# Recurrent step of a four-layer graph network: the tanh of the gates goes to the cell's PSUM bank, and h times c gets a semaphore per half

## The chip, the cores and the metric

The kernel runs on one core of a Trainium2 chip. The metric is the device time in microseconds of one execution, the median of the runs of a kernel. The engines are named as in the profile: PE is TensorE, DVE is VectorE, ACT is ScalarE, POOL is GpSimd, SP is SyncE.

## What is computed

Four layers run one after the other on 6250 rows of 256 features, each as `x = x + layer(layernorm(x))`: a graph attention layer, a mixture of experts, a three-hop graph convolution, and a recurrent layer. The change touches only the recurrent one. It walks over the 6250 rows in order, with a batch of one, a hidden state `h` and a cell `c` of 256 values each:

```python
def step(carry, xs):
    h, c = carry
    xi_t, xf_t, xg_t, xo_t = xs
    i_t = jax.nn.sigmoid(xi_t + h @ V_i)
    f_t = jax.nn.sigmoid(xf_t + h @ V_f)      # not used by c_new
    g_t = jnp.tanh(xg_t + h @ V_c)
    o_t = jax.nn.sigmoid(xo_t + h @ V_o)
    c_new = h * c + i_t * g_t
    h_new = o_t * jnp.tanh(c_new)
    return ((h_new, c_new), h_new)
```

The old cell is multiplied by the old `h`, not by a forget gate. A step needs the `h` of the step before, so nothing of one step's gates can start before the step before has ended.

## The kernel before

`lstm_layer` keeps the 256 hidden values as two halves (`KD` = 2, index `m` or `q`) of 128 partitions by one column. All weights are split into a high and a low fp16 part, and a product takes three terms (high by high, low by high, high by low), so a step has 36 matmuls of 128x128 by 128x1: 24 for the gates `i` and `g` (banks `ZI0`, `ZI1`), then 12 for `o` (banks `ZO..`). `ORDER` sets their order by hand: bank `ZI0` (gates of half 0) is complete after 17 of them, `ZI1` after 24, the two `o` banks after 30 and 36. The parts `x @ U + b` of the next 125 steps are added ahead, one wide matmul after each of the first 48 steps of a group of 125.

The work of a step, half by half, each handed over by a semaphore that counts steps (`t`):

- PE (line 2402) waits for `h1_made[q]` (the high part of half q of `h`) and later `h2_made[q]` (its low part), and raises `z[bank]` with the last matmul of a bank.
- ACT (line 2419) waits for `z[m]` and writes the tanh of both `i/2` and `g` (two columns) to the SBUF tile `tg`; it raises `gates[m]`. The sigmoid of `i` is had from the tanh of half its argument.
- DVE (line 2446) waits for `gates[m]`, in half 0 for `hc_made` too, and makes the new cell by a scan of two columns from `tg` and `one_hc` (the columns 1 and h*c) into columns 0 and 1 of the PSUM tile `c[m]`, a bank for each half; it raises `cell[m]`.
- ACT (lines 2422 and 2424) makes the sigmoid of `o` (waits for `z[2 + m]`), then the tanh of the cell (waits for `cell[m]`), and raises `tanh_made[m]`.
- DVE (line 2451) multiplies the two into `h1`, the fp16 value that PE waits for. Then follow the low part (line 2455), `h` in fp32 (line 2456), and for the next step h*c of half 0 and of half 1 (lines 2458 and 2459), of which the second raises `hc_made`.

Each engine runs its own instructions in the order in which the code is written; the body of the loop is written out for 1250 steps and run five times. POOL copies `h` of 125 steps at a time to a table (line 2358). On steps 0 and 1 of each group of 125, ACT clears half a bank (line 2427).

In the built program an instruction carries one wait. Where the code has two, the wait that is written last becomes an instruction of its own (a semaphore instruction on the same queue) ahead of the one that works, and the wait that is written first stays on the working instruction. Another place with two waits is the expert layer, where one transpose on PE (line 1718) raises `transh`, and both DVE and ACT wait for that same semaphore, DVE with one wait and ACT with two:

```python
                        dve.wait_ge(transh, 2 + 2 * t + n + 1)      # 1771
                        nc.vector.tensor_copy(HT[:, ...], psT[n][:]...)                  # 1772
...
                        act.wait_ge(hid, 2 * t + n + 1)             # 1646, done long before
                        act.wait_ge(transh, 2 * t + n + 1)          # 1647, stands ahead on its own
                        nc.scalar.activation(Hs[:, ...], psH[...][:], ACT.Gelu)          # 1648
```

Of the kernel before, what the change touches and what calls it, by code (L numbers as in the profile page):

```python
# [8 lines left out]
ACT = mybir.ActivationFunctionType  # L9
ALU = mybir.AluOpType  # L10
AXX = mybir.AxisListType.X

P = 128
# [4 lines left out]
KD = D // P  # L18
# [2172 lines left out]
def lstm_layer(nc, k, X, U, V, b, out):  # L2191
# [3 lines left out]
    with Phase(nc, "ls") as ph:  # L2195
# [8 lines left out]
        h = ph.sb("h", [P, RECENT, KD])  # L2204
        h1 = ph.sb("h1", [P, RECENT, KD, 2], F16)
        h2 = ph.sb("h2", [P, RECENT, KD, 2], F16)
        none = ph.sb("none", [P, KD * HALF])
        tg = ph.sb("tg", [P, 2, KD, 2])
        to = ph.sb("to", [P, 2, KD, 2])
        one_hc = ph.sb("one_hc", [P, KD, 2])  # L2210


        with Phase(nc, "lp") as pp:
# [12 lines left out]
            scale = sc[:, 0:1].bitcast(F32)  # L2226
            with pp.block() as block:
                @block.sync
                def _(sp):
                    sp.dma_start(Us[:], U.rearrange("(k p) (m c) -> p k m c", k=KD, c=P)).then_inc(loaded, 16)  # L2230
                    sp.dma_start(Vs[:], V.rearrange("(k p) (m c) -> p k m c", k=KD, c=P)).then_inc(loaded, 16)
                    sp.dma_start(brow[:], b.rearrange("(a m c) -> a m c", a=1, c=P)).then_inc(loaded, 16)
# [103 lines left out]
        with Phase(nc, "lr") as pr:  # L2336
            ZI = [pr.ps(f"ZI{m}") for m in range(KD)]
            ZO = [[pr.ps(f"ZO{i}{m}") for m in range(KD)] for i in range(2)]
            c = [pr.ps(f"c{m}") for m in range(KD)]
            cleared = [pr.sem(f"cleared{m}") for m in range(KD)]  # L2340
            z = [pr.sem(f"z{g}") for g in range(BANKS)]
            gates, cell, tanh_made, h1_made = ([pr.sem(f"{n}{j}") for j in range(KD)] for n in ("gates", "cell", "tanh", "h1_"))
            h2_made = [pr.sem(f"h2_{j}") for j in range(KD)]
            h_made, hc_made, kept = (pr.sem(n) for n in ("h", "hc", "kept"))

            def place(hf, bank, col, count):
                if bank < KD:
                    return ZI[bank][:, hf * KD * HALF + col:hf * KD * HALF + col + count]
                return ZO[hf][bank - KD][:, col:col + count]

            with pr.block() as block:
# [57 lines left out]
                @block.scalar  # L2409
                def _(act):  # L2410
                    back = act.alloc_register("unscale")
                    act.reg_load(back, sc[0:1, 1:2])
                    nc.scalar.preload_act_table(ACT.Sigmoid)
                    with act.Fori(0, N // BODY) as i:
                        for s in range(BODY):
                            hf, col, t = s // HALF % 2, s % HALF * KD, i * BODY + s
                            for m in range(KD):
                                act.wait_ge(z[m], t + 1)
                                nc.scalar.activation(tg[:, s % 2, m, :], place(hf, m, col, 2), ACT.Tanh, scale=back).then_inc(gates[m], 1)  # L2419
                            for m in range(KD):  # L2420
                                act.wait_ge(z[2 + m], t + 1)
                                nc.scalar.activation(to[:, s % 2, m, 1:2], place(hf, KD + m, col, 1), ACT.Sigmoid, scale=back)  # L2422
                                act.wait_ge(cell[m], t + 1)
                                nc.scalar.activation(to[:, s % 2, m, 0:1], c[m][:, 1:2], ACT.Tanh, scale=0.5).then_inc(tanh_made[m], 1)  # L2424
                            if s % HALF < KD:
                                m = s % HALF
                                nc.scalar.copy(place(1 - hf, m, 0, KD * HALF), none[:]).then_inc(cleared[m], 1)

                @block.vector
                def _(dve):  # L2430

                    nc.vector.memset(h1[:, 0:RECENT - 1], 0.0)
                    for m in range(KD):
                        nc.vector.memset(h1[:, RECENT - 1, m], 0.0).then_inc(h1_made[m], 1)
                        nc.vector.memset(h2[:, RECENT - 1, m], 0.0).then_inc(h2_made[m], 1)
                    nc.vector.memset(one_hc[:, :, 0], 1.0)
                    nc.vector.memset(one_hc[:, :, 1], 0.0).then_inc(hc_made, 1)
                    with dve.Fori(0, N // BODY) as i:
                        for s in range(BODY):
                            t, e, r = i * BODY + s, s % 2, s % RECENT  # L2440
                            for m in range(KD):
                                dve.wait_ge(gates[m], t + 1)
                                if m == 0:
                                    dve.wait_ge(hc_made, t + 1)

                                nc.vector.tensor_tensor_scan(c[m][:, 0:2], tg[:, e, m, :], one_hc[:, m, :], 1.0, ALU.mult, ALU.add).then_inc(cell[m], 1)  # L2446
                            if s % HALF == 0:
                                dve.wait_ge(kept, i * (BODY // HALF) + s // HALF + 1)
                            for m in range(KD):
                                dve.wait_ge(tanh_made[m], t + 1)  # L2450
                                nc.vector.tensor_tensor(h1[:, r, m, 1:2], to[:, e, m, 1:2], to[:, e, m, 0:1], ALU.mult).then_inc(h1_made[m], 1)  # L2451

                            for m in range(KD):
                                dve.wait_ge(h1_made[m], t + 2)
                                nc.vector.tensor_tensor_scan(h2[:, r, m, :], to[:, e, m, :], h1[:, r, m, :], 1.0, ALU.mult, ALU.subtract).then_inc(h2_made[m], 1)  # L2455
                            nc.vector.tensor_tensor(h[:, r, :], to[:, e, :, 1], to[:, e, :, 0], ALU.mult).then_inc(h_made, 1)  # L2456
                            dve.wait_ge(h_made, t + 1)
                            nc.vector.tensor_tensor(one_hc[:, 0, 1:2], h[:, r, 0:1], c[0][:, 1:2], ALU.mult)  # L2458
                            nc.vector.tensor_tensor(one_hc[:, 1, 1:2], h[:, r, 1:2], c[1][:, 1:2], ALU.mult).then_inc(hc_made, 1)  # L2459


        with Phase(nc, "lf") as pf:
# [71 lines left out]
def build(nc, x, src, dst, edge_weight, gat_W_src, gat_W_dst, gat_att_src, gat_att_dst, gat_bias, gat_gamma, gat_beta,  # L2534
          gat_prelu, moe_Wr, moe_br, moe_g, moe_b, moe_W1, moe_b1, moe_W2, moe_b2, gnn_WnT, gnn_bn, gnn_WsT, gnn_bs,
          lstm_U, lstm_V, lstm_b, out):
    with Phase(nc, "all") as ph:
        k = Constants(nc, ph)
        X = ph.sb("X", [P, NB, D])
        with ph.block() as block:  # L2540
            @block.vector
            def _(dve):
                nc.vector.memset(X[:, FULL:NB, :], 0.0)
        order = EdgeOrder(nc, "ss", src, dst, edge_weight)
        gat_layer(nc, k, x, X, src, dst, gat_W_src, gat_W_dst, gat_att_src, gat_att_dst, gat_bias, gat_gamma, gat_beta, gat_prelu, order)
        moe_layer(nc, k, X, moe_Wr, moe_br, moe_g, moe_b, moe_W1, moe_b1, moe_W2, moe_b2, order,
                  lambda Y, where, weight: gnn_layer(nc, k, X, order, gnn_WnT, gnn_bn, gnn_WsT, gnn_bs, Y, where, weight))
        lstm_layer(nc, k, X, lstm_U, lstm_V, lstm_b, out)
# [26 lines left out]
```

## Time and profile before

| | us |
|---|---|
| median of three runs | 19581.66 |
| lowest and highest run | 19550.09 and 19586.31 |
| span of the profiled execution, first to last instruction | 17545.4 |
| recurrent loop within that span | about 8147 to 17502 |
| one step of the loop, 6250 of them | 1.48 in most |

The profiled execution is one run; for its own time the profile gives the span alone, and the runs are about 2036 us longer than the span, which lies before the first and behind the last instruction that the profile counts. Engines are busy at the same time, so their shares do not add up. In the rows below, busy time is followed by the mean of one instruction; the last part of a row is how long its engine sat idle before it and what ended that.

### The profile page before, as it was taken

The page shows a single profiled execution, that of the slowest core. Times are in us where ns is not written, and L with a number is a line of the kernel's source. Part 1 is how long each engine was busy: PE and PEld are TensorE (multiplying, and loading weights), DVE is VectorE, ACT ScalarE, POOL GpSimd, SP SyncE. Part 2 cuts the span into 40 slices and gives each one's busy share as a digit, 9 for nine tenths or more (in the row PEclk, how much of TensorE's full clock was granted, in tenths as well). Part 3 has the DMA queues.
Part 4 walks back from the last instruction along what each step waited for, and adds up shares of the span by engine and source line. Part 5 has one row for each costly group of instructions (what it writes and reads, how often), then busy time and mean ns, then how long its engine had stood idle before and what let it go on. Part 6 is the DMA issues. An engine that isn't in the chain of part 4 may idle for free. (4 is left out here: it accounts for less than half of the span.)

```text
span 17545.4 us, 683245 instructions
## 1 busy us (share of the span) xinstructions
PE 12730.7 (73%) x250869; PEld 10213.3 (58%) x250870; DVE 11697.3 (67%) x68713; ACT 5986.8 (34%) x41949; POOL 5631.1 (32%) x6174
## 2 busy tenths in 40 slices
PE   5247773399655656556888888888888888888887
PEld 3135552266444544445777777777777777777776
DVE  7368887322555454556777777777777777777777
ACT  0004442011100101003555555554555555555555
POOL 4778887666576575772000000000000000000000
PEclk6558886599877777775555555555555555555555
DMA  0102222111333333331000000000000000000000
GB/s 22 25 21 73 74 72 43 56 34 33 101 105 98 96 105 87 105 105 37 4 4 4 4 4 4 4 4 4 4 4 4 4 4 4 4 4 4 4 4 18
DMA packets 352412, 609.44 MB, mean 35 GB/s; under 512 B 157501, under 2 KB 232222, under 8 KB 348988
## 3 DMA queue, kind: packets, MB, share of 16 engines
q0 software_dynamic: 223104, 471.33, 10.4%
q1 hardware_dynamic: 126524, 100.27, 1.9%
q8 instruction: 1835, 30.06, 0.7%
q14 instruction: 949, 7.77, 0.1%
HBM read 508.72 MB, written 62.45 MB: 33 GB/s over the span
## 5 line engine op out<-in xcount | busy, mean ns | idle before, releaser
L2402 PE MATMUL lr_ZI<-ls_h,ls_V 128*128 128x1 f16 x150000 | 5006.8, 166 | 1669.7 <-DVE ls_h L2451 1412.8
L2402 PEld LDWEIGHTS lr_ZI<-ls_h,ls_V 128*128 128x128 f16 x150000 | 4487.3, 104 | 2677.0 <-DVE ls_h L2451 2640.4
L2419 ACT ACTIVATE ls_tg<-lr_ZI 128x2 f32<-128x2 f32 x12500 | 2150.0, 172 | 4626.5 <-PE lr_ZI L2402 4534.6
L2446 DVE TENSOR_TENSOR_SCAN lr_c<-ls_tg,ls_one_hc 128x2 f32<-128x2 f32 x12500 | 2118.1, 170 | 1441.0 <-ACT ls_tg L2419 1317.8
L2358 POOL COPY ls_HT<-ls_h 128x250 f32 x50 | 19.8, 395 | 9358.3 <-DVE ls_h L2456 9358.3
L2402 PE MATMUL lr_ZO<-ls_h,ls_V 128*128 128x1 f16 x75000 | 2865.0, 165 | 0.0
L671 PE MATMUL prop_sum<-prop_G,prop_S 128*128 128x256 f32 x4992 | 1830.4, 546 | 1369.9 <-DMA prop_G<-hop_table,prop_idx 1369.9
L657 POOL DMA_INDIRECT prop_G<-hop_table,prop_idx x2496 | 2368.3, 949 | 1057.3 <-issue 708.8
L2402 PEld LDWEIGHTS lr_ZO<-ls_h,ls_V 128*128 128x128 f16 x75000 | 2483.2, 104 | 0.0
L671 PEld LDWEIGHTS prop_sum<-prop_G,prop_S 128*128 128x128 f32 x4992 | 1403.9, 288 | 1796.3 <-issue 1486.1
L2451 DVE TENSOR_TENSOR ls_h<-ls_to 128x1 f16<-128x1 f32 x12500 | 2023.4, 162 | 479.1 <-ACT ls_to L2424 16.0
L2424 ACT ACTIVATE ls_to<-lr_c 128x1 f32<-128x1 f32 x12500 | 2102.5, 169 | 9.9 <-DVE lr_c L2446 1.0
L2422 ACT ACTIVATE ls_to<-lr_ZO 128x1 f32<-128x1 f32 x12500 | 2069.3, 171 | 0.0
L2455 DVE TENSOR_TENSOR_SCAN ls_h<-ls_to,ls_h 128x2 f16<-128x2 f32 x12500 | 1633.5, 162 | 25.7 <-issue 25.7
L694 DVE TENSOR_TENSOR gnn_agg<-gnn_agg,prop_sum 128x256 f32 x1664 | 694.9, 418 | 908.7 <-PE prop_sum L671 884.9
L2458 DVE TENSOR_TENSOR ls_one_hc<-ls_h,lr_c 128x1 f32<-128x1 f32 x6250 | 969.0, 155 | 220.0
L633 ACT CAST prop_idx<-gnn_SRT 128x8 int32 (+1 forms) x312 | 63.3, 203 | 2915.2 <-DMA prop_G<-hop_table,prop_idx 2903.7
L680 DVE TENSOR_SCALAR prop_S<-all_cols,prop_lw 128x128 f32<-128x128 f32 x2520 | 900.5, 358 | 165.6 <-issue 153.3
L2456 DVE TENSOR_TENSOR ls_h<-ls_to 128x2 f32<-128x2 f32 x6250 | 952.9, 152 | 7.2 <-issue 7.2
L2459 DVE TENSOR_TENSOR ls_one_hc<-ls_h,lr_c 128x1 f32<-128x1 f32 x6250 | 930.2, 149 | 0.0
L522 POOL DMA_INDIRECT sd_records<-sc_rec,sc_place x784 | 772.5, 985 | 440.7 <-issue 408.0
L1007 POOL DMA_INDIRECT all_X<-gat_table,gs_idx x832 | 825.3, 992 | 239.1 <-issue 239.1
(455 smaller groups left out, 13965.7 us busy)
## 6 DMA issues: line engine op xcount, KB each, us to landing
prop_G<-hop_table,prop_idx POOLq DMA_INDIRECT x2496, 2.7
mow_W<-in_L_ffn_W SPq DMA_DIRECT2D x16, 1024.0 KB, 10.8
moe_out<-me_Ys SPq DMA_DIRECT2D x108, 128.0 KB, 1.7
all_X<-gat_table,gs_idx POOLq DMA_INDIRECT x832, 2.8
hop_table<-ht_T SPq DMA_DIRECT2D x50, 256.0 KB, 2.1
sd_records<-sc_rec,sc_place POOLq DMA_INDIRECT x784
ss_records<-me_recs,me_places POOLq DMA_INDIRECT x540
gat_table<-gt_hs SPq DMA_DIRECT2D x50, 128.0 KB, 1.8
```

The lines of the kernel that those rows point to most:

```text
L657: nc.gpsimd.indirect_dma_start(out=G[:, r, u, :], out_offset=None, in_=table[:, :], in_offset=bass.IndirectOffsetOnAxis(ap=idx[:, r, u:u + ...
L671: nc.tensor.matmul(ps[u][:, 0:D], S[:, r % 2, u, :], G[:, r, u, :], start=True, stop=True).then_inc(mm, 1)
L2402: mm = nc.tensor.matmul(place(hf, bank, col, 1), (V2 if part == "21" else V1)[:, q, ROWS.index(row), :], hx[:, prev, q, 1:2], start=False, ...
L2419: nc.scalar.activation(tg[:, s % 2, m, :], place(hf, m, col, 2), ACT.Tanh, scale=back).then_inc(gates[m], 1)
L2422: nc.scalar.activation(to[:, s % 2, m, 1:2], place(hf, KD + m, col, 1), ACT.Sigmoid, scale=back)
L2424: nc.scalar.activation(to[:, s % 2, m, 0:1], c[m][:, 1:2], ACT.Tanh, scale=0.5).then_inc(tanh_made[m], 1)
L2446: nc.vector.tensor_tensor_scan(c[m][:, 0:2], tg[:, e, m, :], one_hc[:, m, :], 1.0, ALU.mult, ALU.add).then_inc(cell[m], 1)
L2451: nc.vector.tensor_tensor(h1[:, r, m, 1:2], to[:, e, m, 1:2], to[:, e, m, 0:1], ALU.mult).then_inc(h1_made[m], 1)
L2455: nc.vector.tensor_tensor_scan(h2[:, r, m, :], to[:, e, m, :], h1[:, r, m, :], 1.0, ALU.mult, ALU.subtract).then_inc(h2_made[m], 1)
L2456: nc.vector.tensor_tensor(h[:, r, :], to[:, e, :, 1], to[:, e, :, 0], ALU.mult).then_inc(h_made, 1)
L2458: nc.vector.tensor_tensor(one_hc[:, 0, 1:2], h[:, r, 0:1], c[0][:, 1:2], ALU.mult)
L2459: nc.vector.tensor_tensor(one_hc[:, 1, 1:2], h[:, r, 1:2], c[1][:, 1:2], ALU.mult).then_inc(hc_made, 1)
```

## The change

`tg` goes away. The tanh of the gates is written to columns 2 and 3 (`GATED`) of the same PSUM tile `c[m]` whose columns 0 and 1 (`CELL`) hold the cell, and the scan reads it there. Since ACT now writes a bank that DVE reads in lines 2458 and 2459 (h*c), ACT waits for that h*c before it writes; for this `hc_made` becomes a list of two semaphores, one for each half.

```diff
-        tg = ph.sb("tg", [P, 2, KD, 2])
...
-            h_made, hc_made, kept = (pr.sem(n) for n in ("h", "hc", "kept"))
+            hc_made = [pr.sem(f"hc{j}") for j in range(KD)]
+            h_made, kept = pr.sem("h"), pr.sem("kept")
+            CELL, GATED = slice(0, 2), slice(2, 4)
...
                             for m in range(KD):
+                                act.wait_ge(hc_made[m], t + 1)
                                 act.wait_ge(z[m], t + 1)
-                                nc.scalar.activation(tg[:, s % 2, m, :], place(hf, m, col, 2), ACT.Tanh, scale=back).then_inc(gates[m], 1)
+                                nc.scalar.activation(c[m][:, GATED], place(hf, m, col, 2), ACT.Tanh, scale=back).then_inc(gates[m], 1)
...
                                 dve.wait_ge(gates[m], t + 1)
                                 if m == 0:
-                                    dve.wait_ge(hc_made, t + 1)
-
-                                nc.vector.tensor_tensor_scan(c[m][:, 0:2], tg[:, e, m, :], one_hc[:, m, :], 1.0, ALU.mult, ALU.add).then_inc(cell[m], 1)
+                                    dve.wait_ge(hc_made[KD - 1], t + 1)
+                                nc.vector.tensor_tensor_scan(c[m][:, CELL], c[m][:, GATED], one_hc[:, m, :], 1.0, ALU.mult, ALU.add).then_inc(cell[m], 1)
...
-                            nc.vector.tensor_tensor(one_hc[:, 0, 1:2], h[:, r, 0:1], c[0][:, 1:2], ALU.mult)
-                            nc.vector.tensor_tensor(one_hc[:, 1, 1:2], h[:, r, 1:2], c[1][:, 1:2], ALU.mult).then_inc(hc_made, 1)
+                            for m in range(KD):
+                                nc.vector.tensor_tensor(one_hc[:, m, 1:2], h[:, r, m:m + 1], c[m][:, 1:2], ALU.mult).then_inc(hc_made[m], 1)
```

No working instruction is added, dropped or moved on any engine; what changes is where two of them read and write, and the waits of one. The instructions of ACT for one step stand in the program before like this. A wait is shown under a name that its semaphore's number had in an earlier phase of the program: `gs_primed` is `z[0]`, `gs_ready` is `z[1]`, the others are `z[2]`, `cell[0]`, `z[3]`, `cell[1]`, in that order.

```order
L2418 REGISTER_ALU
L2419 ACTIVATE ls_tg<-lr_ZI0 128x2 [waits gs_primed]
L2419 ACTIVATE ls_tg<-lr_ZI1 128x2 [waits gs_ready]
L2422 ACTIVATE ls_to<-lr_ZO00 128x1 [waits gf_std_made]
L2424 ACTIVATE ls_to<-lr_c0 128x1 [waits gf_step]
L2422 ACTIVATE ls_to<-lr_ZO01 128x1 [waits gf_var_made]
L2424 ACTIVATE ls_to<-lr_c1 128x1 [waits gf_loaded]
```

The same step on ACT in the changed program; `mr_centred` is `hc_made[0]` and `mr_taken` is `hc_made[1]`. Of two names the first is the wait that stands as an instruction of its own ahead, the second is carried by the instruction shown.

```order
L2419 REGISTER_ALU
L2421 ACTIVATE lr_c0<-lr_ZI0 128x2 [waits gs_primed,mr_centred]
L2421 ACTIVATE lr_c1<-lr_ZI1 128x2 [waits gs_ready,mr_taken]
L2424 ACTIVATE ls_to<-lr_ZO00 128x1 [waits gf_std_made]
L2426 ACTIVATE ls_to<-lr_c0 128x1 [waits gf_step]
L2424 ACTIVATE ls_to<-lr_ZO01 128x1 [waits gf_var_made]
L2426 ACTIVATE ls_to<-lr_c1 128x1 [waits gf_loaded]
```

What moved is the wait for `z[m]`: from the tanh itself to a semaphore instruction ahead of it, while the new wait for h*c sits on the tanh. On DVE the new cell had two waits before and has them still, in the same places; `mr_taken` is `hc_made` of the kernel before, `gf_returned` and `gf_made` are `gates[0]` and `gates[1]`. Five instructions of DVE around it in the program before:

```order
L2456 TENSOR_TENSOR ls_h<-ls_to 128x2
L2458 TENSOR_TENSOR ls_one_hc<-ls_h,lr_c0 128x1 [waits mr_centred]
L2459 TENSOR_TENSOR ls_one_hc<-ls_h,lr_c1 128x1
L2446 SCALAR_TENSOR_TENSOR lr_c0<-ls_tg,ls_one_hc 128x2 [waits mr_taken,gf_returned]
L2446 SCALAR_TENSOR_TENSOR lr_c1<-ls_tg,ls_one_hc 128x2 [waits gf_made]
```

And in the changed program, where the same number on the first h*c has another old name (`h_made` in both):

```order
L2458 TENSOR_TENSOR ls_h<-ls_to 128x2
L2461 TENSOR_TENSOR ls_one_hc<-ls_h,lr_c0 128x1 [waits mr_prods]
L2461 TENSOR_TENSOR ls_one_hc<-ls_h,lr_c1 128x1
L2448 SCALAR_TENSOR_TENSOR lr_c0<-lr_c0,ls_one_hc 128x2 [waits mr_taken,gf_returned]
L2448 SCALAR_TENSOR_TENSOR lr_c1<-lr_c1,ls_one_hc 128x2 [waits gf_made]
```

Here nothing moved: the wait for h*c of half 1 stands alone ahead, and the wait for the gates is on the scan. (The scan is called SCALAR_TENSOR_TENSOR in this list and TENSOR_TENSOR_SCAN in the profile.)

## Rows read from the trace of the kernel before

**Rows 1.** The page: span, and granted TensorE clock in tenths, 40 slices
```profile
span 17545.4 us, 683245 instructions
...
PEclk6558886599877777775555555555555555555555
```

**Rows 2.** Waits in the loop, 8147.3 to 17502: total us, times, longest
```profile
ACT ls_tg L2419 <- PE lr_ZI L2402: 4534.6, 6250, 10.1
...
DVE lr_c L2446 <- ACT ls_tg L2419: 1317.8, 6105, 11.4
...
DVE ls_h L2455 <- issue: 25.7, 100, 0.3
```

**Rows 3.** Timeline of one step, all engines: start us, us, engine, line, what
```profile
12001.15 0.35 DVE L2451 TENSOR_TENSOR ls_h<-ls_to 128x1 f16<-128x1 f32 x2
...
12001.37 0.80 PE L2402 MATMUL lr_ZI<-ls_h,ls_V 128*128 128x1 f16 x24 [0.36 <-DVE ls_h L2451]
...
12001.80 0.16 DVE L2458 TENSOR_TENSOR ls_one_hc<-ls_h,lr_c 128x1 f32<-128x1 f32 x1
12001.87 0.15 DVE L2459 TENSOR_TENSOR ls_one_hc<-ls_h,lr_c 128x1 f32<-128x1 f32 x1
...
12002.02 0.36 ACT L2419 ACTIVATE ls_tg<-lr_ZI 128x2 f32<-128x2 f32 x2 [0.71 <-PE lr_ZI L2402]
...
12002.22 0.36 DVE L2446 TENSOR_TENSOR_SCAN lr_c<-ls_tg,ls_one_hc 128x2 f32<-128x2 f32 x2 [0.20 <-ACT ls_tg L2419]
12002.36 0.17 ACT L2422 ACTIVATE ls_to<-lr_ZO 128x1 f32<-128x1 f32 x1
12002.43 0.17 ACT L2424 ACTIVATE ls_to<-lr_c 128x1 f32<-128x1 f32 x1
...
12002.61 0.17 ACT L2424 ACTIVATE ls_to<-lr_c 128x1 f32<-128x1 f32 x1
12002.63 0.35 DVE L2451 TENSOR_TENSOR ls_h<-ls_to 128x1 f16<-128x1 f32 x2
...
12002.85 0.48 PE L2402 MATMUL lr_ZI<-ls_h,ls_V 128*128 128x1 f16 x12 [0.36 <-DVE ls_h L2451]
```

**Rows 4.** Line 2419: count, ns min/median/max, first and last start
```profile
L2419 ACT ACTIVATE ls_tg<-lr_ZI x12500: 172/172/173, 8147.3 to 17500.3; 128x2 f32<-128x2 f32 x199
```

**Rows 5.** Timeline of the expert layer, two places
```profile
3962.35 0.69 DVE L1772 COPY me_HT<-me_T 128x512 f32<-128x512 f32 x1 [1.75 <-PE me_T L1718]
3962.41 0.60 ACT L1648 ACTIVATE me_H<-me_H 128x512 f32<-128x512 f32 x1 [2.16 <-PE me_T L1718]
...
4397.55 0.69 DVE L1772 COPY me_HT<-me_T 128x512 f32<-128x512 f32 x1 [1.67 <-PE me_T L1718]
4397.61 0.60 ACT L1648 ACTIVATE me_H<-me_H 128x512 f32<-128x512 f32 x1 [2.27 <-PE me_T L1718]
```

**Rows 6.** Groups of ACT by line and shape: busy us, mean ns
```profile
L954 ACT CAST gs_ST<-gs_T 128x512 bf16<-128x512 f32 x208 | 110.8, 583 | 4.8 <-PE gs_T L1047 4.8
...
L2324 ACT COPY lp_xT<-lp_T 128x256 f32<-128x256 f32 x49 | 18.3, 373 | 12.5 <-PE lp_T L2307 11.6
L2087 ACT COPY co_idx<-moe_where 128x2 int32<-128x2 int32 x50 | 6.7, 183 | 12.3 <-PEq L72 12.3
...
L2427 ACT COPY lr_ZI<-ls_none 128x250 f32<-128x250 f32 x100 | 37.5, 375 | 0.0
```

**Rows 7.** Groups of DVE by line and shape: busy us, mean ns
```profile
L2446 DVE TENSOR_TENSOR_SCAN lr_c<-ls_tg,ls_one_hc 128x2 f32<-128x2 f32 x12500 | 2118.1, 170 | 1441.0 <-ACT ls_tg L2419 1317.8
...
L2455 DVE TENSOR_TENSOR_SCAN ls_h<-ls_to,ls_h 128x2 f16<-128x2 f32 x12500 | 1633.5, 162 | 25.7 <-issue 25.7
...
L1901 DVE TENSOR_TENSOR all_X<-all_X,ht_S 128x256 f32<-128x256 f32 x50 | 20.9, 420 | 54.9 <-PE ht_S L1975 54.9
...
L1147 DVE COPY gs_top<-gs_fin 128x4 f32<-128x4 f32 x104 | 19.0, 183 | 3.6
...
L772 DVE COPY gt_A<-gt_H 128x8 f32 x46 | 7.1, 154 | 0.0
...
L1906 DVE TENSOR_TENSOR ht_b<-ht_b 128x256 f32<-128x256 f32 x2 | 0.9, 426 | 12.3 <-DMA ht_b<-in_gnn_bs 12.3
```

More of the change, by code:

```diff
@@ L2436, in _ @@
                     nc.vector.memset(one_hc[:, :, 0], 1.0)
-                    nc.vector.memset(one_hc[:, :, 1], 0.0).then_inc(hc_made, 1)
+                    for m in range(KD):
+                        nc.vector.memset(one_hc[:, m, 1:2], 0.0).then_inc(hc_made[m], 1)
                     with dve.Fori(0, N // BODY) as i:
@@ L2457, in _ @@
                             dve.wait_ge(h_made, t + 1)
-                            nc.vector.tensor_tensor(one_hc[:, 0, 1:2], h[:, r, 0:1], c[0][:, 1:2], ALU.mult)
-                            nc.vector.tensor_tensor(one_hc[:, 1, 1:2], h[:, r, 1:2], c[1][:, 1:2], ALU.mult).then_inc(hc_made, 1)
+                            for m in range(KD):
+                                nc.vector.tensor_tensor(one_hc[:, m, 1:2], h[:, r, m:m + 1], c[m][:, 1:2], ALU.mult).then_inc(hc_made[m], 1)
         with Phase(nc, "lf") as pf:
```

## The prediction

> **What bounds the kernel now.** I read the page first: the span is 17545 us, and in its last 22 of 40 slices nothing of the granted clock changes; TensorE is granted 0.5 there, its lower level of 1.2 GHz [rows 1]. That stretch is the recurrent loop: its first and last tanh of the gates start at 8147.3 and 17500.3 us [rows 4], so 9353 us for 6250 steps, 1.497 us each, more than half of the span. The page's chain that ended last covers only the final addition and says nothing of the loop, so the waits come next: before every one of the 6250 steps ACT sits idle for PE (4534.6 us in total, 0.73 each), and DVE sits idle for ACT's tanh (1317.8 us) [rows 2]. No engine is full; a step is a chain of hand-overs. The timeline of one step shows it [rows 3]: DVE makes the two halves of the fp16 `h` from 12001.15 on; PE starts at 12001.37 with 24 matmuls, which run in 0.80 us; ACT starts the two tanhs at 12002.02 while the second bank is still being summed; DVE makes the cell from 12002.22 on; ACT does the sigmoids of `o` and the tanhs of the cell from 12002.36 on; DVE makes `h` again at 12002.63. From 12001.15 to 12002.63 is 1.48 us. PE takes 0.65 of it (12001.37 to 12002.02) and the four hand-overs ACT, DVE, ACT, DVE the rest. Every nanosecond added to the tanh of half 0 or to the scan behind it is therefore added to each step; the same holds for half 1, which runs 0.18 us behind in the same pattern, since PE needs it for its ninth matmul. The rest of 1.497 over 1.48 are longer steps, a few of them with DVE idle on issue (100 times, 25.7 us in total) [rows 2].
>
> One number decides whether the new wait can matter by itself. The h*c of half 0 starts at 12001.80 and lasts 0.16, so it is there at 12001.96, that of half 1 at 12001.87 + 0.15 = 12002.02, and the tanhs of the two halves start at 12002.02 and, 0.36 for two of 0.172 apart, at 12002.20 [rows 3, 4]. The h*c of each half is early by 0.06 and 0.18 us. So nothing has to wait for it for long; what it costs is the form in which the wait is built.
>
> **The change part by part.**
>
> *The wait of ACT.* In the changed program the tanh carries the wait for h*c, and the wait for `z[m]`, the one that comes last, stands ahead as an instruction of its own. Then ACT must first retire the semaphore instruction when `z[m]` rises and only then can bring up the tanh. The trace has that situation in the expert layer: DVE's copy and ACT's gelu wait for the same semaphore of the same transpose, DVE on the instruction and ACT on an instruction ahead of it. DVE starts at 3962.35 and 4397.55, ACT at 3962.41 and 4397.61 [rows 5], 0.06 us later in both; at a resolution of 0.01 I take 0.057. The opposite case is in the loop: the scan of half 0 has two waits as well, but there the one that stands ahead (h*c) has come long before. It starts at 12002.22, 0.03 behind the end of the tanh of half 0 (12002.02 + 0.172 = 12002.19), and the second scan, which has one wait, ends the pair at 12002.58 after a start at 12002.41, 0.03 behind the end of its tanh at 12002.38 [rows 3, 4, 7]. So a wait ahead is free when it is already met and costs 0.057 when it is the last. Bounds: 0 (as on that scan) and twice 0.057 (if the halves queued up behind each other). I take 0.057 once: the semaphore instruction of half 1 stands behind the tanh of half 0, which starts some 0.1 us before `z[1]` comes, so each half pays it, but side by side. Behind ACT's wait stand the sigmoid of `o` and the tanh of the cell; the sigmoid waits for PE, starts at 12002.36 now and has 0.16 us from the second tanh, so 0.04 more on that does not move it [rows 3]. On the wide matmuls that wait for `gates[m]` the delay falls into PE's idle time of 0.36 [rows 3].
>
> The Trainium skill ("Perfetto Trace Analysis", Identifying Dependency Chains) says that instructions which wait for several engines may have semaphore instructions put ahead of them. It gives no price; the trace agrees that the second wait is a thing of its own, by the 0.06 of [rows 5].
>
> *The tanh writes to PSUM.* No small instruction of ACT in the trace writes PSUM. The nearest is the clearing copy, SBUF to PSUM, 250 columns, 375 ns; PSUM to SBUF of 256 columns takes 373, of 512 columns 583, which makes 0.82 ns a column; SBUF to SBUF of 2 columns takes 183 [rows 6]. Without their columns: 375 - 205 = 170 to PSUM, 373 - 210 = 163 from PSUM, 183 - 2 = 181 for SBUF on both sides. So a PSUM destination in place of SBUF is worth 11 ns. Bounds: 0 (the wide copies differ by 2 ns only) and 18, the worth of a PSUM source. I take 11.
>
> The Trainium skill ("ScalarE: Activation LUTs", Step-by-step: what each stage is for) calls PSUM the destination of lower latency for ScalarE. It has no figure for it; the rows agree in sign, with the 11 ns above.
>
> *The scan reads PSUM.* An addition of 256 columns with one operand in PSUM takes 420 ns, one with both in SBUF 426; small copies take 154 from PSUM (8 columns) and 183 in SBUF (4 columns); against it, the scan that writes PSUM takes 170 where the one that writes SBUF takes 162, so PSUM is not the near side of DVE in every case [rows 7]. Bounds: 29 ns less and 8 more. I take 6 less, by the additions, which like the scan have two operands.
>
> *The semaphores of h*c.* DVE's first h*c now raises one itself. It is one increment by an instruction that is there already, and it lies in DVE's pause before the scan (0.20 idle) [rows 3]: nothing. That `tg` loses its two alternating buffers costs nothing either, since ACT reaches the next tanh only after it has waited for `cell[m]`, thus for the scan that read them. ACT has two more instructions to fetch per step, seven becoming nine; it sits idle 0.71 in each step, so a fetch is hidden. DVE has as many as before, PE too.
>
> *Sum.* 57 - 11 - 6 = 40 ns a step; times 6250 steps is 250 us. The profiled span would go from 17545 to 17795. The 2036 us that lie between the span and the median of the runs, 19581.66, are not touched, so the forecast is 19581.66 + 250 = 19832 us, 1.3% slower. Its own range: with no help from PSUM and 8 ns against, 65 ns, 406 us, 19988; with half of the price paid back (57 - 18 - 6 = 33 ns, 206 us) 19788; with all the help of the rows, 57 - 18 - 29 = 10 ns, 63 us, 19644.
>
> **The rivals.** From the measurement, about 0.2% (39 us, 6 ns a step) can be told from no change.
>
> *Faster: the wait ahead is hidden, PSUM pays.* If ACT brought the tanh up while the wait for `z[m]` is still open, as it seems on the first scan, the hop would be 0 and only the PSUM terms would be left: -17 ns, -106 us, 19476. It decides from the point where the hop costs less than the PSUM terms (17 to 47 ns). For it: the first scan's 0.03. Against it: that scan's leading wait was met long before, and where it is the last one, both places of [rows 5] show 0.06. 12 in 100.
>
> *No change: PSUM pays for the hop.* If both PSUM terms are at or near their far bounds, 47 ns, what is left is 10 ns or less; a scan that gains some more from reading and writing one bank would bring it to within 6 ns. The time would be 19582 to 19621. For it: the small copies differ by 29. Against it: the additions differ by 6. 9 in 100.
>
> *Slower still: both hops in a row.* If the semaphore instruction of half 1 could start only after the tanh of half 0 has been finished and not merely begun, half 1 would fall behind by a second 57 ns, and PE's ninth matmul and all behind would wait for it: 114 - 17 = 97 ns, 606 us, 20188. Against it: tanhs already start 0.18 apart with a length of 0.17, and half 1 of the chain has no need to be brought up earlier than 0.18 behind [rows 3, 4]. 4 in 100.
>
> **How the numbers follow.** Forecast with its own range (19644 to 19988) 75, faster 12, no change 9, slower still 4. The likeliest gives 19832. For 8 times in 10 the range goes from 19630, a little beyond the far bound of the PSUM terms, to 19990. Faster by over 0.2%: 12; within: 9; slower: 79.
>
> **What would show it.** In the changed profile the tanh of the gates should start about 0.057 later after PE's 24 matmuls began (now 0.65, then 0.71), the mean length of a tanh should fall from 172 to about 161, the scan from 170 to about 164, and a step should take 1.52 where it takes 1.48. The idle time of ACT for PE should rise by the hop, 0.057 a step, from 4534.6 to about 4890 us. PE's and DVE's parts should be the same. A step shorter than 1.48 would make the first term wrong, one over 1.57 the claim that the halves pay side by side. If the tanh's start has moved by 0.06 and the step has not grown, the two PSUM terms are mis-sized.

## The result

The changed kernel takes 19937.82 us in the median of four runs (19932.72 to 19945.11), the kernel before 19576.99 (19550.09 to 19586.31): a ratio of 1.0188, 95% interval 1.0174 to 1.0201. That is 361 us slower, 58 ns for each of the 6250 steps. The forecast was 19832, its range 19630 to 19990. Two of the eleven executions of experiment e1 below, at 19197 and 27441 us, were slow ones; every comparison here is of fast runs alone.

The page of the changed kernel, its span and the granted clock. Here the span is the time of the run but for 2 us, and in the loop, the last half of the slices, the clock is 0.5 as before:

```profile
span 19931.0 us, 695616 instructions
...
PEclk6555777657997676676655555555555555555555
```

The waits of the changed kernel in its loop (total us, times, longest), which answer to [rows 2]:

```profile
ACT lr_c L2421 <- PE lr_ZI L2403: 4925.4, 6254, 10.2
...
DVE lr_c L2448 <- ACT lr_c L2421: 1703.3, 6350, 11.5
ACT lr_c L2421 <- DVE ls_one_hc L2461: 82.8, 96, 0.9
```

ACT's idle time for PE has grown by 390.8 us and DVE's for ACT by 385.5 us; it is one loss, seen from two engines, and about what the kernel lost. The wait for h*c is the last one 96 times only. The tanh, the semaphore instruction ahead of it and the scan of the changed kernel (ns min/median/max, first and last start), which answer to [rows 4, 7]:

```profile
L2421 ACT ACTIVATE lr_c<-lr_ZI x12500: 157/157/157, 10159.4 to 19885.8; 128x2 f32<-128x2 f32 x199
...
L2420 ACTq EVENT_SEMAPHORE  x12500: 17/17/17, 10159.3 to 19885.7; - x199
...
L2448 DVE TENSOR_TENSOR_SCAN lr_c<-lr_c,ls_one_hc x12500: 157/170/170, 10159.6 to 19886.0; 128x2 f32<-128x2 f32 x199
```

The tanh takes 157 ns where it took 172; the scan takes 170 as before. From the first tanh to the last are 9726.4 us, against 9353.0 in [rows 4]: the loop lost 373 us. It starts at 10159 instead of 8147, though nothing ahead of it was changed; the section on the prediction comes back to that. One step of the changed kernel, which answers to [rows 3]:

```profile
14009.88 0.35 DVE L2453 TENSOR_TENSOR ls_h<-ls_to 128x1 f16<-128x1 f32 x2
14010.10 0.80 PE L2403 MATMUL lr_ZI<-ls_h,ls_V 128*128 128x1 f16 x24 [0.41 <-DVE ls_h L2453]
...
14010.53 0.22 DVE L2461 TENSOR_TENSOR ls_one_hc<-ls_h,lr_c 128x1 f32<-128x1 f32 x2
...
14010.82 0.34 ACT L2421 ACTIVATE lr_c<-lr_ZI 128x2 f32<-128x2 f32 x2 [0.78 <-PE lr_ZI L2403]
14011.01 0.36 DVE L2448 TENSOR_TENSOR_SCAN lr_c<-lr_c,ls_one_hc 128x2 f32<-128x2 f32 x2 [0.26 <-ACT lr_c L2421]
14011.10 0.17 ACT L2424 ACTIVATE ls_to<-lr_ZO 128x1 f32<-128x1 f32 x1
14011.21 0.17 ACT L2426 ACTIVATE ls_to<-lr_c 128x1 f32<-128x1 f32 x1
...
14011.41 0.35 DVE L2453 TENSOR_TENSOR ls_h<-ls_to 128x1 f16<-128x1 f32 x2
```

PE's first matmul to ACT's tanh is now 0.72 us, it was 0.65; a step (14009.88 to 14011.41, from DVE's product for `h1` to the next one) is 1.53, it was 1.48. The h*c of both halves is done at 14010.75, before the tanh starts. One more thing is to be read here: before, the tanh of the cell followed 0.07 behind the sigmoid of `o`; now it follows 0.11 behind it (14011.10 to 14011.21).

The trace also records when each semaphore rises. Times between such a record and the start of an instruction are given in ns below, as the median over the steps unless said otherwise. The tanh of half 0 starts 22 ns after `z[0]` rises in the kernel before and 88 ns after it in the changed one. That difference of some 65 ns is called the hop.

### The profile page after: what moved, and what is told of

Its sections match the earlier page's. It is cut to its first block and busy times, and to the rows that moved or that the text cites. A ratio compares the mean times of both kernels' runs of the same rounds, so it can differ in the third digit from the quotient of the medians.

```text
span 19931.0 us, 695616 instructions
## 1 busy us (share of the span) xinstructions
PE 13009.4 (65%) x250738; PEld 10113.7 (51%) x250870; DVE 11651.9 (58%) x68714; ACT 5778.6 (29%) x41949; POOL 5613.9 (28%) x6174
## 5 line engine op out<-in xcount | busy, mean ns | idle before, releaser
L2421 ACT ACTIVATE lr_c<-lr_ZI 128x2 f32<-128x2 f32 x12500 | 1955.4, 157 | 5187.8 <-PE lr_ZI L2403 4925.4
L2448 DVE TENSOR_TENSOR_SCAN lr_c<-lr_c,ls_one_hc 128x2 f32<-128x2 f32 x12500 | 2106.5, 170 | 1808.2 <-ACT lr_c L2421 1703.3
L671 PEld LDWEIGHTS prop_sum<-prop_G,prop_S 128*128 128x128 f32 x4992 | 1184.3, 259 | 2569.0 <-issue 2210.8
L2461 DVE TENSOR_TENSOR ls_one_hc<-ls_h,lr_c 128x1 f32<-128x1 f32 x12500 | 1385.6, 152 | 220.1
L638 ACT COPY prop_lw<-gnn_SRT 128x16 f32 (+1 forms) x315 | 64.4, 205 | 3472.5 <-DVE prop_S L680 2800.8
L1068 PE MATMUL gs_O<-gs_M,gs_S 128*128 128x260 f32 x1664 | 686.8, 503 | 138.9 <-issue 64.6
```

The lines of the kernel that those rows point to most:

```text
L671: nc.tensor.matmul(ps[u][:, 0:D], S[:, r % 2, u, :], G[:, r, u, :], start=True, stop=True).then_inc(mm, 1)
L2421: nc.scalar.activation(c[m][:, GATED], place(hf, m, col, 2), ACT.Tanh, scale=back).then_inc(gates[m], 1)
L2448: nc.vector.tensor_tensor_scan(c[m][:, CELL], c[m][:, GATED], one_hc[:, m, :], 1.0, ALU.mult, ALU.add).then_inc(cell[m], 1)
L2461: nc.vector.tensor_tensor(one_hc[:, m, 1:2], h[:, r, m:m + 1], c[m][:, 1:2], ALU.mult).then_inc(hc_made[m], 1)
```

## The experiments

All eight ran against the kernel before, which took 17554 us beside the first four (e1 to e4) and 17551 beside the last four, not 19577. The step of 1.48 us is read from the profiled run of the kernel before, whose span of 17545 us belongs to these times. The last column is of one profiled run each; single runs of the kernel before lie between 17544 and 17561 us, so differences of some 15 us in it mean nothing.

| run | what | ratio (95%) | us against before | loop, first to last tanh |
|---|---|---|---|---|
| kernel before, profile of before | | | | 9353.0 |
| e1 | one more wait, always met early | 1.0010 (1.0000 to 1.0019) | +13 | 9364.9 |
| e2 | the same, `z[m]` ahead | 1.0257 (1.0243 to 1.0271) | +454 | 9807.9 |
| e3 | changed kernel, waits swapped | 1.0034 (1.0021 to 1.0048) | +62 | 9422.0 |
| e4 | tanh in PSUM, in `ZI[m]` | 1.0005 (0.9996 to 1.0014) | +9 | 9365.0 |
| e5 | before, one `o` matmul less | 0.9996 (0.9987 to 1.0005) | -7 | 9368.0 |
| e6 | e4, one `o` matmul less | 0.9959 (0.9946 to 0.9973) | -70 | 9288.2 |
| e7 | changed kernel again | 1.0208 (1.0194 to 1.0222) | +369 | 9729.9 |
| e8 | e3 with an early h*c | 1.0002 (0.9993 to 1.0011) | +3 | 9366.2 |

### e1 and e2: the same two waits in both orders

The edit of e1 to the kernel before; e2 has the added line above the other one:

```diff
                                 act.wait_ge(z[m], t + 1)
+                                act.wait_ge(h2_made[m], t + 1)
```

> The kernel before, with one more wait on each tanh of the gates, on h2_made[m], written behind the wait for z[m], so that it stands ahead as an instruction of its own. h2_made of both halves comes some 0.29 us before z[0], so this wait is always met early. Theory (only a wait that comes last is dear when it stands ahead): the step stays at 1.48 us; two more instructions of ACT per step cost at most the 6 ns a step by which the changed kernel's mean outgrew its median, so 19577 to 19617. Rival (a second wait costs its 60 ns wherever it stands): 19577 + 6250 x 0.060 = about 19950.

> The same kernel as the one with the met wait, instruction for instruction, but with the wait for h2_made[m] written first, so that the wait for z[m], which comes last, stands ahead. The tanh still goes to SBUF. Theory: the whole loss of the changed kernel is this position, and its PSUM tile gives 15 ns a step back (tanh 172 to 157 ns): so this one is slower than the changed kernel, by 0.065 x 6250 = 406 us for the hop and up to 40 us for the two more instructions: 19980 to 20025. Rival (the loss comes from the PSUM bank or from waiting for h*c): near 19577.

Measured: e1 +13 us, e2 +454. The two kernels have the same instructions on every engine and differ in which of two waits stands ahead. Their tanhs and what follows, e1 first, both from the timeline:

```profile
12001.76 0.80 PE L2402 MATMUL lr_ZI<-ls_h,ls_V 128*128 128x1 f16 x24 [0.36 <-DVE ls_h L2452]
...
12002.41 0.36 ACT L2420 ACTIVATE ls_tg<-lr_ZI 128x2 f32<-128x2 f32 x2 [0.71 <-PE lr_ZI L2402]
```

```profile
12001.39 0.36 ACT L2420 ACTIVATE ls_tg<-lr_ZI 128x2 f32<-128x2 f32 x2 [0.78 <-PE lr_ZI L2402]
...
12001.67 0.17 ACT L2423 ACTIVATE ls_to<-lr_ZO 128x1 f32<-128x1 f32 x1
12001.80 0.17 ACT L2425 ACTIVATE ls_to<-lr_c 128x1 f32<-128x1 f32 x1
```

In e1 ACT's idle time before the tanh is 0.71 us, as without the extra wait [rows 3]; in e2 it is 0.78. By the semaphore records the tanh starts 23 ns after `z[0]` in e1 and 89 in e2, in the changed kernel 88. So the extra wait costs at most a few ns a step where the one ahead is met early (33 us at the end of the interval are 5 ns), and about 65 ns where the one ahead is the last to come: shown. It costs that once, not once a half: twice would have been over 800 us. And e2, with the hop and without the PSUM tile, is slower than the changed kernel in e7 by 454 - 369 = 85 us, 14 ns a step; that is close to the 15 ns by which the tanh is shorter when it writes PSUM.

### e3 and e8: the changed kernel with its waits in the other order

```diff
-                                act.wait_ge(hc_made[m], t + 1)
                                 act.wait_ge(z[m], t + 1)
+                                act.wait_ge(hc_made[m], t + 1)
```

> The changed kernel with the two waits of the tanh in the other order: z[m] first, then hc_made[m], so that the wait for h*c stands ahead. In the changed trace the semaphore of half 0's h*c comes only about 32 ns before z[0]; the semaphore instruction needs 21 ns to start and the tanh follows 67 ns behind it, so the tanh of half 0 can start 56 ns after z[0], where it is 88 in the changed kernel and 23 in the one before. Theory (position of the wait that comes last, and this latency): +33 for the rest of the hop, -15 for the tanh, -3 in the tanh of the cell, +6 for the longer queue = +21 ns a step, 130 us, about 19705. Rival A (a wait written last is free if it is met at all by z[m]): -12 ns a step, about 19500. Rival B (the order is not what costs): about 19940.

Measured: +62 us, half of the theory's 130 and far from both rivals. The swap alone takes back 307 of the 369 us. The tanh of e3:

```profile
12001.22 0.80 PE L2403 MATMUL lr_ZI<-ls_h,ls_V 128*128 128x1 f16 x24 [0.36 <-DVE ls_h L2453]
...
12001.63 0.22 DVE L2461 TENSOR_TENSOR ls_one_hc<-ls_h,lr_c 128x1 f32<-128x1 f32 x2
...
12001.89 0.32 ACT L2421 ACTIVATE lr_c<-lr_ZI 128x2 f32<-128x2 f32 x2 [0.75 <-PE lr_ZI L2403]
12002.08 0.34 DVE L2448 TENSOR_TENSOR_SCAN lr_c<-lr_c,ls_one_hc 128x2 f32<-128x2 f32 x2 [0.22 <-ACT lr_c L2421]
12002.21 0.17 ACT L2424 ACTIVATE ls_to<-lr_ZO 128x1 f32<-128x1 f32 x1
12002.28 0.17 ACT L2426 ACTIVATE ls_to<-lr_c 128x1 f32<-128x1 f32 x1
```

It starts 0.67 us after PE's first matmul (0.65 before, 0.72 changed). It is 37 ns after `z[0]`, where it is 22 in the kernel before and 88 in the changed one; 56 had been expected. The semaphore of h*c, which now stands ahead, rises 52 ns before `z[0]` here, against 33 in the changed kernel, and the tanh starts 89 ns after it: the wait ahead still decides, only by less. Of the 62 us, some 44 are in longer steps: what exceeds the common 1.480 us by over 60 ns adds up to 148 us in the trace of e3, to 104 in that of the kernel before.

One rule gives the start of the tanh in the kernels with two waits. It starts 88 ns after the semaphore that stands ahead or 22 ns after the one it carries, whichever is later. In e1, e2, e3, e8 and the changed kernel this holds within 2 ns in 99% of the steps or more for half 0. So by these traces the wait ahead must be met 66 ns before the other to cost nothing; 52 are not enough.

e8 takes the lateness of h*c away (the swap stays). It makes h*c straight from the sigmoid of `o`, the tanh and the cell, so DVE's wait for `h_made` goes too:

```diff
+                            for m in range(KD):
+                                nc.vector.scalar_tensor_tensor(one_hc[:, m, 1:2], to[:, e, m, 1:2], to[:, e, m, 0:1], c[m][:, 1:2], ALU.mult, ALU.mult).then_inc(hc_made[m], 1)
                             nc.vector.tensor_tensor(h[:, r, :], to[:, e, :, 1], to[:, e, :, 0], ALU.mult).then_inc(h_made, 1)
-                            dve.wait_ge(h_made, t + 1)
-                            for m in range(KD):
-                                nc.vector.tensor_tensor(one_hc[:, m, 1:2], h[:, r, m:m + 1], c[m][:, 1:2], ALU.mult).then_inc(hc_made[m], 1)
```

> The changed kernel with the waits swapped (z[m] first, hc_made[m] second, so that h*c stands ahead), and h*c made in one instruction, (sigmoid of o times tanh of the cell) times c, ahead of h in fp32, so that it does not wait for h_made and comes some 0.2 us earlier. Theory (what was left of the loss with swapped waits is the lateness of h*c, 32 ns before z[0]): the tanh of the gates starts 23 ns after z[0] again, the PSUM gain is swallowed behind the sigmoid of o, and the step is 1.480 us as in the kernel before: 0 to +40 us against it. Rival (the leftover is the price of two semaphore instructions or of the shared bank): +61 us as with the swapped waits alone.

Measured: +3 us, as the theory had it. The timeline of e8:

```profile
12000.97 0.80 PE L2403 MATMUL lr_ZI<-ls_h,ls_V 128*128 128x1 f16 x24 [0.36 <-DVE ls_h L2453]
...
12001.19 0.33 DVE L2459 SCALAR_TENSOR_TENSOR ls_one_hc<-ls_to,lr_c 128x1 f32<-128x1 f32 x2
...
12001.61 0.34 ACT L2421 ACTIVATE lr_c<-lr_ZI 128x2 f32<-128x2 f32 x2 [0.73 <-PE lr_ZI L2403]
```

h*c is done at 12001.52 and the tanh starts 0.64 us after PE's first matmul. Its semaphore rises 180 ns before `z[0]`, and the tanh starts 23 ns after `z[0]`; it takes 157 ns and the scan 170, as in the changed kernel. So neither the two semaphore instructions nor the shared bank show a cost of their own: all of the changed kernel's loss goes when no wait ahead of the tanh comes late. But all of it, and no more: the 15 ns of the shorter tanh are not seen in the time.

### e4, e5 and e6: where the shorter tanh's gain goes

e4 leaves the cell's bank alone and puts the tanh into spare columns of the bank it is read from; one wait is enough there:

```diff
+            GATED = slice(2 * KD * HALF, 2 * KD * HALF + 2)
...
-                            pe.wait_ge(gates[bank], t + 1)
+                            pe.wait_ge(cell[bank], t + 1)
...
-                                nc.scalar.activation(tg[:, s % 2, m, :], place(hf, m, col, 2), ACT.Tanh, scale=back).then_inc(gates[m], 1)
+                                nc.scalar.activation(ZI[m][:, GATED], place(hf, m, col, 2), ACT.Tanh, scale=back).then_inc(gates[m], 1)
...
-                                nc.vector.tensor_tensor_scan(c[m][:, 0:2], tg[:, e, m, :], one_hc[:, m, :], 1.0, ALU.mult, ALU.add).then_inc(cell[m], 1)
+                                nc.vector.tensor_tensor_scan(c[m][:, 0:2], ZI[m][:, GATED], one_hc[:, m, :], 1.0, ALU.mult, ALU.add).then_inc(cell[m], 1)
```

> The kernel before, with tanh written to PSUM but to two spare columns of the bank ZI[m] that it reads, not of the cell's bank; DVE reads it there. ACT needs no wait for h*c, so it has one wait as before; PE's wide matmuls into ZI[m] wait for cell[m] in place of gates[m]. Theory: the tanh's 15 ns are all that PSUM gives, the scan's read gives nothing, and PE's later wait is in its idle time: -15 ns a step, -94 us, about 19485. Rival (the PSUM tile itself costs, or the later wide matmuls hold up PE): 19577 or more.

Measured: +9 us, within the interval no difference. My theory of 94 us gained fell. Its timeline shows where they went:

```profile
12001.36 0.80 PE L2402 MATMUL lr_ZI<-ls_h,ls_V 128*128 128x1 f16 x24 [0.36 <-DVE ls_h L2451]
...
12002.01 0.34 ACT L2419 ACTIVATE lr_ZI<-lr_ZI 128x2 f32<-128x2 f32 x2 [0.73 <-PE lr_ZI L2402]
12002.19 0.36 DVE L2446 TENSOR_TENSOR_SCAN lr_c<-lr_ZI,ls_one_hc 128x2 f32<-128x2 f32 x2 [0.20 <-ACT lr_ZI L2419]
12002.35 0.17 ACT L2422 ACTIVATE ls_to<-lr_ZO 128x1 f32<-128x1 f32 x1
12002.42 0.17 ACT L2424 ACTIVATE ls_to<-lr_c 128x1 f32<-128x1 f32 x1
```

The scan starts 0.18 us after the tanh (0.20 in [rows 3]) and is over at 12002.36. But the tanh of the cell starts at 12002.42, 0.06 later, where a hand-over from DVE takes 0.03. It stands behind the sigmoid of `o` in ACT's queue and follows it by 0.07, as in [rows 3] (12002.36 and 12002.43), and that sigmoid starts when PE has done `z[2]`, 30 matmuls after the step began. In the kernel before, too, that is what the tanh of the cell waits for. It starts 29 ns after `cell[0]` rises there, and 45 ns in e4, where 22 to 23 is the usual hand-over: the path through the first tanh and the scan has 7 ns to spare before and 22 in e4. e5 and e6 take one matmul before `z[2]` out, from the kernel before and from e4:

```diff
-         + [t for row in ("o0", "o1") for q in range(KD) for t in terms(row, "11 21 12", q)])
+         + [t for row in ("o0", "o1") for q in range(KD) for t in terms(row, "11 21 12", q) if t != ("o0", "21", 1)])
```

> The kernel before without one of the 36 matmuls of a step, the last low-by-high product of gate o, half 0 (that product is left out of the result), so that bank ZO of half 0 is complete after 29 matmuls instead of 30, 27 ns earlier; z[0] and z[1] stay as they are. Theory (from the runs so far): in the kernel before, the tanh of the cell of half 0 starts 68 ns behind the sigmoid of o in front of it on ACT, and that sigmoid waits for z[2]; the cell itself is there some 7 ns earlier than needed. So with the sigmoid 27 ns earlier the step can gain no more than the 7 ns: -44 us. Rival A (the chain through the cell alone bounds a step): 0. Rival B (the matmuls before z[2] bound it alone): -27 ns, -168 us.

> The kernel with the tanh in spare columns of ZI[m], without the same matmul of gate o (its product is left out of the result). There the cell of half 0 is ready 45 ns before the tanh of the cell starts, of which 23 is the usual hand-over: 22 ns lie unused. Theory (the 15 ns that the PSUM destination saves were swallowed by the wait behind the sigmoid): with the sigmoid out of the way the step gains 22 ns, -138 us against the kernel before, and 15 ns (94 us) more than the same cut brings without the PSUM tile. Rival (the shorter tanh is of no use anywhere): the same as the cut without the PSUM tile.

Measured: e5 -7 us (interval -23 to +9), e6 -70 (-95 to -47). The timeline of e6:

```profile
12002.59 0.34 ACT L2419 ACTIVATE lr_ZI<-lr_ZI 128x2 f32<-128x2 f32 x2 [0.72 <-PE lr_ZI L2402]
12002.78 0.36 DVE L2446 TENSOR_TENSOR_SCAN lr_c<-lr_ZI,ls_one_hc 128x2 f32<-128x2 f32 x2 [0.19 <-ACT lr_ZI L2419]
12002.91 0.17 ACT L2422 ACTIVATE ls_to<-lr_ZO 128x1 f32<-128x1 f32 x1
12002.98 0.17 ACT L2424 ACTIVATE ls_to<-lr_c 128x1 f32<-128x1 f32 x1
```

Here the tanh of the cell starts 0.03 behind the end of the scan (12002.95), and 0.39 behind the first tanh instead of 0.41. The same cut gives nothing with `tg` in SBUF and 63 us, 10 ns a step, more with the tile in PSUM: the shorter tanh is worth something as soon as the sigmoid is out of the way. Both came out smaller than I had them. In e5 the sigmoid no longer sits right in front: the tanh of the cell starts 90 ns behind it instead of 67, and 4 ns earlier after the first tanh. But it takes longer. Line 2424 in the kernel before and in e5:

```profile
L2424 ACT ACTIVATE ls_to<-lr_c x12500: 166/171/180, 8147.7 to 17500.7; 128x1 f32<-128x1 f32 x199
...
L2424 ACT ACTIVATE ls_to<-lr_c x12500: 171/171/180, 8143.6 to 17511.6; 128x1 f32<-128x1 f32 x199
```

For half 0 it is 166 ns in nearly all steps before, right behind the sigmoid, and 171 in e5. That takes back what was gained. In e6 the trace has 17 ns between `z[0]` and the first half of `h` saved, of which 3 are lost from `h` to the next `z[0]` (672 to 675), and a step fell by 13, from 1.480 to 1.467. e6 is the only version that beats the kernel before, and it leaves a product of the result out, so it is no candidate; a version that computes all and gains was not found. One way would be the `o` matmuls of half 0 before the gates of half 1, which makes half 1 later; it was not tried.

### e7: the changed kernel beside the other time of the kernel before

No edit.

> The changed kernel as it is, timed beside the kernel before where that takes 17554 us. The first comparison was 361 us at 19577. Theory (all of the difference is in the recurrent loop, 6250 steps of 60 ns more, the 2 ms between the two times of the kernel before are in the layers ahead of it): 17554 + 361 to 373 = about 17920. Rival (a part of it is proportional to the whole time): 17554 x 1.0188 = 17884 or less.

Measured: 17919.63 us, +369, ratio 1.0208. The difference stays while the whole time is 2 ms less, so it is not proportional to it. The tanh of e7, whose first start shows that the loop begins where it did in [rows 4]:

```profile
L2421 ACT ACTIVATE lr_c<-lr_ZI x12500: 157/157/157, 8145.0 to 17874.9; 128x2 f32<-128x2 f32 x199
```

## Why the prediction was right, and where it was not

**The bound and the first term held.** A step is a chain of hand-overs, the tanh is on it, and the wait for `z[m]` that stands ahead is what costs. Predicted 57 ns, measured some 65 (ACT's idle time 0.71 to 0.78 us; 22 to 88 ns after `z[0]` by the semaphore records). The term came out 8 ns small because [rows 5] set a gelu against a copy on another engine: by the records of the same trace the gelu starts 82 to 83 ns after its semaphore and the copy 24, where the tanh starts 88 and 22 after. The wait's twin in the loop, free because it is met early, was read rightly: e1.

**Halves side by side.** Right: e2 has one hop, not two. The rival of both hops in a row is out.

**The tanh to PSUM.** Predicted 11 ns, the tanh is 15 ns shorter, 172 to 157. The Trainium skill ("ScalarE: Activation LUTs", Step-by-step: what each stage is for), which calls PSUM the nearer destination of ScalarE, agrees with this. In the changed kernel it is paid out nearly in full (e2 against e7, 14 ns): the tanh of the cell starts 23 ns after `cell[0]` there, with nothing to spare, because the hop has made the cell late. In the kernel before it is worth nothing (e4, e8).

**The scan from PSUM.** Predicted 6 ns less, measured none: 170 both times. The additions of 256 columns do not carry over to a scan of two.

**How early h*c is.** The prediction had half 0's h*c early by 0.06 us, from the end of the instruction. Its semaphore rises 33 ns before `z[0]` in the changed kernel. With `z[0]` ahead that is enough, as predicted; with h*c ahead it is not (e3).

**The step that failed: the tanh of the cell.** The prediction said that the sigmoid of `o` has 0.16 us to spare behind the second tanh and dropped it. What it missed is the instruction behind the sigmoid. The tanh of the cell follows 0.07 after it in [rows 3] and is bound by it, not by the cell: e4, e5 and e6 show this, since the shorter tanh and the earlier sigmoid give next to nothing alone and 13 ns a step together. So of a hop of 65 ns some 7 are absorbed, and of a gain on the tanh nothing arrives. The rival "faster: the wait ahead is hidden, PSUM pays" had this wrong as well: e8 is that case, and where it had 17 ns a step less, 106 us, the time was 3 us more.

**What was costed at nothing.** In the changed kernel the common step grew by 53 ns, from 1.480 to 1.533 us, but the mean by 373 / 6250 = 60. The other 7 ns, some 40 us, are in longer steps: in those over 60 ns above the common one, the excess adds up to 144 us in the trace of the changed kernel and to 104 in that of before. The 96 waits of ACT for h*c are new, yet e2 has as much (140 us) without them, and e1, with the same count of instructions, has 112. So the queue's length alone does not make it. The excess goes with a late wait ahead: 140 to 148 us in the four traces that have one (changed, e2, e3, e7), 103 to 122 in the others (before, e1, e4, e5, e6, e8). By what way is open.

**The sum.** 65 for the hop, -15 for the tanh, -7 absorbed behind the sigmoid, +6 for the longer tanh of the cell, +4 from the first `h` to `z[0]` (672 to 676 ns by the semaphore records, not explained), +7 in long steps is 60 ns, 375 us, where 40 ns and 250 us were predicted. That the time fell within the range is in part luck: its upper end, 65 ns a step, was drawn for a PSUM destination that gives nothing, and the measured 60 comes about otherwise, with that gain there and with 10 ns of terms that were not in the sum.

**A wrong statement ahead of the prediction.** The 2036 us between the span of the profiled run and the median do not lie around the span. The kernel before has two times, 19577 and 17551 to 17554 us, and the profiled run had the shorter one. The difference lies in the layers ahead of the loop: the same changed kernel starts its loop at 10159 us in its first profile and at 8145 in e7. For the kernel before there is a trace of the shorter time only (8147). As the change is in the loop alone, the difference of 40 ns a step could be added to either. Why the earlier layers take 2 ms more in some sets of runs was not studied. It is not one layer alone: the first transpose of the expert layer on PE (line 1718) is at 4703 us against 3508 in e7, the first gather of the graph convolution (line 657) at 6072 against 4620.

## What to carry to other kernels

When an instruction needs two semaphores, find out which of the two stands as an instruction of its own ahead, and let that be the one that comes early: here the order of two lines was worth 307 us, and the extra wait itself next to nothing. Early means early enough, here 66 ns: 52 still cost something (e3), 180 did not (e8). Before crediting a shorter instruction on a chain, look at what else its successor stands behind in its own engine's queue. A gain of 15 ns on a path that has 7 ns to spare already is not a gain; the path then has 22 ns to spare, and the time is the same (e4).

## What the runs showed that I had not expected

A tanh of two columns on ACT takes 172 ns from PSUM to SBUF and 157 from PSUM to PSUM, in each of 12500 instructions. In most kernels here most steps have one of a few lengths: 1.467 (e6), 1.480 (before, e1, e4, e8), 1.487 (over a third of e5's profiled run), 1.533 (changed), 1.547 us (e2), with few between them; they lie 7 ns or a multiple of it apart, at a granted clock of 0.5 throughout. e3 is the exception: most of its steps spread over 1.479 to 1.489. Such fixed lengths could let gains of a few ns vanish or count double; that, and the cause, were not tested.
